# An opening without diagonals: where a graph-attention kernel makes its first norms, sums and shifts

## The reference

```
h  = relu(layernorm(x))
s  = (h @ W) @ a1 + ((ent @ W) @ a2).T          # 4096 x 4096
e  = where(adj > 0, leaky_relu(s, 0.2), -9e15)
x  = x + elu(softmax(e, axis=1) @ ent + h)
h  = relu(layernorm(x))
out = x + (adj == 1) @ h + h
```

## Time and profile before

| | us |
|---|---|
| median of 3 runs | 394.81 |
| lowest, highest | 394.11, 399.67 |
| profiled execution | 395.57 |
| its span in the profile | 393.8 |
| TensorE busy | 347.1 |
| VectorE busy | 302.9 |
| ScalarE busy | 189.3 |
| GpSimd busy | 123.8 |

### The profile page before, as it was taken

How to read it: one execution, slowest core, us unless ns; L and a number is a source line. 1 busy time by engine, 2 the same in 40 slices (tenths; PEclk the granted TensorE clock), 3 DMA queues, 4 the chain that set the end, 5 groups by cost and what they waited for, 6 DMA issues and landing times.

```text
span 393.8 us, 5685 instructions
## 1 busy us (share of the span) xinstructions
PE 347.1 (88%) x2327; PEld 122.8 (31%) x2327; DVE 302.9 (77%) x334; ACT 189.3 (48%) x241; POOL 123.8 (31%) x164
## 2 busy tenths in 40 slices
PE   1598397999867988899897999998989999999996
PEld 0345111223211221233222433332323333334564
DVE  2813889999889998989899589899897898922211
ACT  1131255776556655635745555445656555522100
POOL 4299993111111114134511311111114399000400
PEclk9989879999999999999998999999999999999999
DMA  7999969999797966765699567999999960000011
GB/s 208 257 213 213 213 126 212 213 213 214 151 136 128 160 124 106 146 108 90 117 135 153 95 112 95 109 108 108 107 103 107 107 68 2 0 2 2 1 55 53
DMA packets 15850, 47.92 MB, mean 122 GB/s; under 512 B 1553, under 2 KB 1617, under 8 KB 15569
## 3 DMA queue, kind: packets, MB, share of 16 engines
q0 software_dynamic: 14656, 44.05, 72.0%
q1 hardware_dynamic: 1168, 3.52, 2.5%
HBM read 111.53 MB, written 1.05 MB: 286 GB/s over the span
## 4 chain that ended last, share of the span: by engine, by line
PE 43%; DVE 16%; issue 5%; ACT 3%; POOL 1%; DVEq 0%; ACTq 0%
PE pb L1161 14%; PE pb L1082 9%; PE pa L1082 8%; PE pb L1176 8%; DVE yp L870 7%; DVE am L780 5%; ACT yp L642 2%; PE pa L1053 1%; PE pa L978 1%; PE pa L1047 1%; POOL rstd L497 1%; DVE gmax L742 1%; PE pa L1043 1%; DVE ta L811 1%; DVE ta L810 1%
## 5 line engine op out<-in xcount | busy, mean ns | idle before, releaser
L642 ACT ACTIVATE yp<-yp,tbias 128x1024 f32<-128x1024 f32 (+1 forms) x160 | 151.6, 977 | 109.7 <-DVE yp L870 108.4
L870 DVE SCALAR_TENSOR_TENSOR yp<-s8b,t8neg,am 128x1024 f32<-128x1024 f32 (+1 forms) x160 | 164.6, 1076 | 20.2 <-PE pb L1176 19.0
L1161 PE MATMUL pb<-yp,enta 128*64 128x512 f32 x512 | 138.0, 622 | 26.4 <-ACT yp L642 26.2
L422 POOL DMA_DIRECT2D am<-adj_t x64 | 35.2, 557 | 126.9 <-DVE yp L870 126.6
L780 DVE TENSOR_TENSOR am<-am,vx 128x4096 uint16<-128x4096 uint16 x32 | 73.5, 2298 | 1.2 <-ACT vx L556 1.2
L1176 PE MATMUL pb<-yp,onesf 128*32 128x512 f32 x512 | 68.5, 607 | 0.0
L1161 PEld LDWEIGHTS pb<-yp,enta 128*64 128x64 f32 x512 | 28.6, 137 | 93.2 <-ACT yp L642 68.0
L1082 PE MATMUL pb<-am,h 128*64 128x512 bf16 (+1 forms) x432 | 55.8, 383 | 0.0
L1082 PEld LDWEIGHTS pb<-am,h 128*64 128x64 bf16 x432 | 26.5, 111 | 40.3 <-issue 29.6
L431 POOL DMA_DIRECT2D am<-adj_t x16 | 11.5, 717 | 61.4 <-DVE yp L870 61.4
L1082 PE MATMUL pa<-am,h 128*64 128x512 fp8e4 x240 | 28.2, 380 | 0.0
(11 more groups left out here) (160 smaller groups left out, 254.9 us busy)
## 6 DMA issues: line engine op xcount, KB each, us to landing
am<-adj_t POOLq DMA_DIRECT2D x80, 512.0 KB, 9.7
edge<-adj_t POOLq DMA_DIRECT2D x4, 512.0 KB, 9.8
enta<-ent SPq DMA_DIRECT2D x1, 1040.0 KB, 5.3
xs<-xt SPq DMA_DIRECT2D x1, 1024.0 KB, 11.8
out<-yp SPq DMA_DIRECT2D x4, 256.0 KB, 2.0
mats<-eye SPq DMA_DIRECT2D x1, 320.0 KB, 7.3
wt_sb<-w_t SPq DMA_DIRECT2D x1, 32.0 KB, 2.2
a_sb<-a_cols SPq DMA_DIRECT2D x1, 0.5 KB, 2.0
```

The costliest lines, as they stand in the source:

```text
L422: pool.dma_start(am[:, q % RING], adj_t[q]).then_inc(landed[q % RING], 16)
L642: e = sc.activation(y, y, ACT.Exp, bias=tbias[:, at:at + 1])
L870: y = v.scalar_tensor_tensor(out=yp[:, n % YS, r * HALF:r * HALF + W], in0=s8b[:, pair(b) % 2, cols(b)], scalar=t8neg[:, at:at + 1], in1=a ...
L1161: t.matmul(acc2(b)[s * D:(s + 1) * D, :], enta[:, at, 0:D], yp[:, n % YS, s * HALF:(s + 1) * HALF], start=(jt == 0), stop=final, tile_posi ...
```

## The change

- `spread_out` becomes `deviations_first`: GpSimd makes the root alone, no diagonals. `deviation` on TensorE now multiplies the root's column, repeated 64 times as weights, by the identity: eight products of 128 columns for a pair instead of two of 512 columns. The squares go to a part of `h3` (`sq0`) instead of `yp`, so that the steps may use `yp` while they are needed.
- The norms of pairs 2 and 3 move. Their centring and variance stand behind `v_rows(0, 0)`, mixed with the sums `biggest(1, 0..2)`; their `deviation` in steps 1 and 3, and their `normed` behind `y` of steps 4 and 6 (`NORM`). The banks of `pb` are assigned anew (`bank_n`), and the denominators' first product waits for `normed(1)`.
- The column sums of the entities are made in three parts (`column_sums`), two products ahead of `biggest(0, 7)`, three ahead of `turn(0, 0)` and three ahead of `v_rows(0, 0)`, in a bank of their own (`esums`). `turn(0, 0)` no longer waits for their copy.
- GpSimd issues chunks 4 to 17 at once, then makes the roots of pairs 0 and 1, issues chunks 18 to 23, makes the roots of pairs 2 and 3, and then splits the sums.
- Block 1's sums: `biggest(1, 0..2)` stand ahead of step 0, and the estimate of landing changes, so that k = 3 falls on step 0, and k = 4 to 7 on steps 1 to 4 (before: k = 0 to 4 on step 0, and 5 to 7 on steps 1 to 3). `read_sums(1)` moves from step 4 to step 5, and turn, largest, shifts and rows of block 1 each by one step.
- `LONE_AT` goes from 6 to 12, and `lone_rows` of block 1 on VectorE no longer waits for block 0's products.

The diff, cut to its core:

```diff
-        n = max(0, int(q * 1.29 - 15.5)) if q < 32 else 0
+        n = min(24, max(0, int(q * 1.27 - 14.2))) if q < 32 else 0
...
-    LONE_AT = 6
+    LONE_AT = 12
+    NORM = {2: dict(dev=1, h=4), 3: dict(dev=3, h=6)}
...
+        def bank_n(p):
+            return pb[:, (2, 0, 1, 3)[p]]
+        esums = pb[:, 3, 0:4 * (D + 1)]
... GpSimd
-            def spread_out(p):
+            def deviations_first(p):
                 pool.wait_ge(var0_sb, p + 1)
                 link(g.tensor_scalar(rstd0[:, p], rstd0[:, p], 1.0, EPS, ALU.mult, ALU.add))
-                link(g.tensor_tensor(rstd0[:, p], rstd0[:, p], mhalf[:], ALU.pow))
-                g.tensor_tensor(yp[:, p].rearrange("p (t k) -> p t k", k=P),
-                                eyef.unsqueeze(1).to_broadcast([P, 2 * SUB, P]),
-                                rstd0[:, p].unsqueeze(2).to_broadcast([P, 2 * SUB, P]), ALU.mult).then_inc(sd_ready, 1)
-            for q in range(4, 8):
+                g.tensor_tensor(rstd0[:, p], rstd0[:, p], mhalf[:], ALU.pow).then_inc(sd_ready, 1)
+            for q in range(4, 18):
                 load(q)
-            for p in range(NP):
-                spread_out(p)
-                for q in range(8 + 2 * p, 10 + 2 * p):
-                    load(q)
-            for q in range(16, 18):
+            deviations_first(0)
+            deviations_first(1)
+            for q in range(18, RING):
                 load(q)
+            deviations_first(2)
+            deviations_first(3)
... (the split of the sums)
-            for q in range(18, RING):
-                load(q)
... ScalarE
+            for p in range(2):
+                squares_first(p)
+                variances_first(p)
             s_rows(0)
             s_cols(range(0, 1))
+            v_rows(0, 0)
             act.wait_ge(esum_ps, 1)
-            sc.copy(ta[:, 0:4 * (D + 1)], turned[:, 0:4 * (D + 1)]).then_inc(esum_sb, 1)
-            v_rows(0, 0)
+            sc.copy(ta[:, 0:4 * (D + 1)], esums).then_inc(esum_sb, 1)
+            for p in range(2, NP):
+                squares_first(p)
+                variances_first(p)
... VectorE
-                if b >= 1:
+                if b >= 2:
                     dve.wait_ge(pv_done, start_of[b - 1] + LONE_AT + 2)
...
+                for p, f in NORM.items():
+                    if n == f["h"]:
+                        normed(p)
... TensorE
-                for s in range(2):
-                    mm = t.matmul(pb[s * D:(s + 1) * D, p], onesf[:, 0:D], yp[:, p, s * HALF:(s + 1) * HALF],
-                                  start=True, stop=True, tile_position=(0, s * D))
+                for c in range(SUB):
+                    for s in range(2):
+                        k = s * SUB + c
+                        mm = t.matmul(bank_n(p)[s * D:(s + 1) * D, c * P:(c + 1) * P],
+                                      rstd0[:, p, k:k + 1].to_broadcast([P, D]), eyef,
+                                      start=True, stop=True, tile_position=(0, s * D))
...
+            def column_sums(places):
+                for k in places:
+                    mm = t.matmul(esums, onesf[:], enta[:, 4 * k:4 * k + 4].rearrange("p t d -> p (t d)"),
+                                  start=(k == 0), stop=(k == NT // 4 - 1))
... (the new order; only its lines)
             centred_first(0)
             centred_first(1)
             variance(0)
+            pe.wait_ge(gtab_ready, 1)
+            biggest(0, 0)
             variance(1)
+            biggest(0, 1)
             deviation(0)
+            biggest(0, 2)
             s_rows(0)
             s_cols(0)
+            biggest(0, 3)
             deviation(1)
+            for k in range(4, NQ - 1):
                 biggest(0, k)
+            column_sums(range(0, 2))
+            biggest(0, NQ - 1)
+            column_sums(range(2, 5))
             turn(0, 0)
+            column_sums(range(5, NT // 4))
             v_rows(0, 0)
+            biggest(1, 0)
+            centred_first(2)
+            centred_first(3)
+            biggest(1, 1)
+            variance(2)
+            biggest(1, 2)
+            variance(3)
... (in the steps, behind the products of step n)
+                for p, f in NORM.items():
+                    if n == f["dev"]:
+                        deviation(p)
...
-                    if jt == 1 and b >= 1:
-                        pe.wait_ge(den_sb, 2 * b)
+                    if jt == 1:
+                        if b >= 1:
+                            pe.wait_ge(den_sb, 2 * b)
+                        else:
+                            pe.wait_ge(h0_ready, 2)
```

More of the change, by code:

```diff
@@ L231, in graph_layers @@
         arep = am[0:D, 22].bitcast(F32)[:, 0:P]
+        sq0 = h3[:].rearrange("p t d -> p (t d)").bitcast(F32)[:, 0:NP * HALF].rearrange("p (q i) -> p q i", i=HALF)
         def chunks_of(p, j):
@@ L611, in move_out, with squares_first, variances_first @@
                 sc.copy(part[:, k], pb[:, 3]).then_inc(part_ready, 1)
-            for p in range(NP):
+            def squares_first(p):
                 act.wait_ge(x0_ps, p + 1)
-                sc.activation(yp[:, p, 0:HALF], pb[:, p], ACT.Square).then_inc(x0_sq, 1)
-                sc.activation(h0[:, p], pb[:, p], ACT.Relu).then_inc(x0_relu, 1)
+                sc.activation(sq0[:, p], bank_n(p), ACT.Square).then_inc(x0_sq, 1)
+                sc.activation(h0[:, p], bank_n(p), ACT.Relu).then_inc(x0_relu, 1)
+            def variances_first(p):
                 act.wait_ge(var0_ps, p + 1)
@@ L691, in normed @@
                 dve.wait_ge(x0_relu, p + 1)
-                v.tensor_tensor(h0[:, p], h0[:, p], pb[:, p], ALU.mult).then_inc(h0_ready, 1)
+                v.tensor_tensor(h0[:, p], h0[:, p], bank_n(p), ALU.mult).then_inc(h0_ready, 1)
             dve.wait_ge(ld_w, 32)
@@ L849, in _ @@
             read_sums(0)
-            normed(2)
             largest(0, 0)
@@ L854, in _ @@
             lone_rows(0)
-            normed(3)
             for n in range(STEPS_ALL):
@@ L927, in variance @@
                     pe.wait_ge(var0_sb, p)
+                if p >= 2:
+                    pe.wait_ge(vx_ready, 1)
                 for c in range(SUB):
                     at = (p * SUB + c) * 2
-                    mm = t.matmul(rowp[:, at:at + 2], yp[:, p, c * P:(c + 1) * P], mean2, start=True, stop=True)
+                    mm = t.matmul(rowp[:, at:at + 2], sq0[:, p, c * P:(c + 1) * P], mean2, start=True, stop=True)
                 mm.then_inc(var0_ps, 1)
@@ L945, in s_rows @@
                 if p == 0:
-                    pe.wait_ge(var0_sb, NP)
+                    pe.wait_ge(var0_sb, 2)
                     pe.wait_ge(gtab_ready, 1)
@@ L986, in turn @@
                 pe.wait_ge(s8_ready, 2 * (pair(b) + 1))
-                if b == 0:
-                    pe.wait_ge(esum_sb, 1)
-                else:
+                if b >= 1:
                     pe.wait_ge(um_ready, first[b])
@@ L1002, in v_rows @@
                     pe.wait_ge(vx_ready, 1)
+                    pe.wait_ge(var0_sb, NP)
                 for c in range(SUB):
@@ L1088, in neighbours @@
                     mm.then_inc(piece_done, 1)
+            def column_sums(places):
+                for k in places:
+                    mm = t.matmul(esums, onesf[:], enta[:, 4 * k:4 * k + 4].rearrange("p t d -> p (t d)"),
+                                  start=(k == 0), stop=(k == NT // 4 - 1))
+                if NT // 4 - 1 in places:
+                    mm.then_inc(esum_ps, 1)
             def centred_first(p):
-                t.matmul(pb[:, p], centre, xs[:, p], start=True, stop=True).then_inc(x0_ps, 1)
+                if p == 3:
+                    pe.wait_ge(esum_sb, 1)
+                t.matmul(bank_n(p), centre, xs[:, p], start=True, stop=True).then_inc(x0_ps, 1)
             pe.wait_ge(ld_eye, 16)
@@ L1104, in _ @@
             variance(0)
-            centred_first(2)
+            pe.wait_ge(gtab_ready, 1)
+            biggest(0, 0)
             variance(1)
-            centred_first(3)
-            variance(2)
-            variance(3)
+            biggest(0, 1)
             deviation(0)
-            pe.wait_ge(gtab_ready, 1)
-            for k in range(2):
-                biggest(0, k)
+            biggest(0, 2)
             s_rows(0)
             s_cols(0)
[L1116 to L1123, removed]
+            biggest(0, 3)
             deviation(1)
-            for k in range(3, NQ):
+            for k in range(4, NQ - 1):
                 biggest(0, k)
-            deviation(2)
+            column_sums(range(0, 2))
+            biggest(0, NQ - 1)
+            column_sums(range(2, 5))
             turn(0, 0)
+            column_sums(range(5, NT // 4))
             v_rows(0, 0)
-            deviation(3)
+            biggest(1, 0)
[5 more added lines that the diff above has]
+            variance(3)
             for n in range(STEPS_ALL):
@@ L1133, in _ @@
                 for b2 in range(1, NB):
-                    for k in range(NQ):
```

(1 more changed line is left out.)

## The result

The changed kernel takes 393.4 us at the median of 18 runs (391.78 to 396.14), the kernel before 395.93 over as many. The ratio is 0.9936, 95% interval 0.9906 to 0.9965: 2.5 us faster, where 2.9 was forecast; the time itself lies 1.5 above the forecast 391.9. Of the 18 times before, ten lie between 394.11 and 396.55 and eight between 398.88 and 400.70 (the ratio counts only the two of these under 400); the changed kernel has no such second group, and against the ten alone it is 1.8 us faster in the mean (394.95 and 393.13). The profiled execution has a span of 391.6 us against 393.8.

A forecast was written before the change was run, and what follows sets the result against it. VectorE was taken as the bound, a queue behind the first `y`. That starts 6.25 us earlier, less 1.2 of added products and waits of VectorE: 2.9 gained at the tenth `y`, 391.9 against median 394.81; range 388.5 to 397.5.

The forecast's parts named there:

- What bounds it and where the gain ends: Whole kernel: VectorE works off a queue behind the first `y`; 6.25 us earlier there, 2.9 left at tenth `y` and end.
- The diagonals: Pair 0's norm: without diagonals the root is ready at 22.05 instead of 24.0; the new `deviation` takes 1.3 us.
- The path to the largest sums: Opening, from pair 0's root to `read_sums(0)`: the landing at 30.2 sets `biggest(0, 7)`; 31.0 instead of 36.71.
- The rival for the low clock: Opening and loop: TensorE at half clock makes small products dearer; gain between 1.5 and -2, 395 us; chance 10%.
- The first steps: Steps 0 to 9: VectorE waits 1.1 before the fifth `y`, 2.1 before `read_sums(1)`, and does two products of 0.6.
- rival 1: Roots of pairs 2 and 3 held off by VectorE's scores: fifth `y` 3.1 us later, 395.0 us; chance 13%.
- its variant: Roots of pairs 2 and 3: a running root also holds VectorE, 2 x 1.67 us, giving 395.2 us; chance 3%.
- rival 4: Opening: GpSimd's queue doesn't hold so many loads, so `biggest(0, 7)` comes 12.5 us later, 404.4 us; chance 7%.
- The loads: Chunk 18 issued by 27 us instead of 56.24, closing a 3.2 us gap; nobody on the path waits, costed at nothing.
- the step that failed: `lone_rows` at step 12: the same products six steps later, waiting for the split; costed at nothing.

The follow-up runs named there:

- e2: Changed kernel with both deviations and products of pairs 2 and 3 finished ahead of step 0 again; median 397.91 us.
- e1: Changed kernel with the deviations of pairs 2 and 3 in steps 5 and 7, their VectorE products in 8 and 10; median 393.82 us.
- e4: Changed kernel plus eight unused bf16 products in TensorE's wait for the first exponential; median 392.43 us.
- e5: Changed kernel with the old landing estimate, so `read_sums(1)` is in step 4 again; median 394.46 us.
- e6: Changed kernel with chunks 18 to 23 issued behind the split of the sums and after `y` of step 5; median 393.38 us.
- e9: Changed kernel with `LONE_AT` 12 for block 0 only and 6 for the other blocks; median 393.09 us.
- e10: Changed kernel with `LONE_AT` 6 behind block 0 and eight unused products in TensorE's wait for the first exponential; median 391.20 us.
- e11: e10 with the deviations of pairs 2 and 3 in steps 5 and 7, their VectorE products in 8 and 10; median 390.22 us.
- e8: Changed kernel with GpSimd's diagonals and the old `deviation` again for pairs 0 and 1; median 398.95 us.
- e12: e11 plus unused products from 4.7 us on in TensorE's waits through the opening; median 389.59 us.
- e3: Changed kernel with the entities' column sums in one block ahead of `biggest(0, 3)` instead of three parts; median 400.48 us.
- e7: Changed kernel plus eighteen unused products of ones while TensorE waits for its first data, from 4.7 us on; median 394.38 us.

## Why the prediction was right

*What bounds it and where the gain ends.* Right. The first `y` moved by 5.7 us (forecast 6.25), 2.14 were left at the tenth `y` (2.9), and 2.2 at the end. e2 gives the same from the other side. How near the number came is in part luck, as two profiles are compared: the same opening list put the first `y` between 38.50 and 41.33 in eight profiles (changed, e1, e4, e5, e6, e9, e10 and e11), with chunk 7 landing between 29.9 and 30.3 in all of them. That spread is the clock's.

*The diagonals.* Right: root ready near 22.3, pitch at full clock 1.02, the lower bound; I had taken 1.3. e8 shows what they cost: 1.0 of start, and at least 2.3 in the times.

*The path to the largest sums.* The term mis-sized is the clock. I had the landing at 30.2 setting the time and 31.05 for `read_sums(0)`; it came at 32.05, because TensorE worked at the low level until 26.7, and ran `biggest(0, 7)` 1.3 us behind the landing (30.2, as I had it). In e4, e6, e9 and e11, where the clock rose at 18 to 19, the same list gave 30.55 to 30.93. The rival for the low clock was there with a chance of 10%; a part of it happened. From `read_sums(0)` to the first `y` it took 7.95 and not 8.4, which gave back 0.45 of the 1.0.

*The first steps.* Two terms were off and cancelled, which is luck. The fifth `y` waited 2.55, not 1.1, since I counted the loop at full clock; e4, which keeps it, measured 1.1. `read_sums(1)` waited 0.6, not 2.1, as VectorE came later to it; in e11, where it came early, it waited 2.0. Their sum is 3.15, forecast 3.2. The two products on VectorE cost 0.6 each, as said.

*GpSimd.* Right. Its operations for pairs 2 and 3 took 0.75, 2.05, 0.43 and 2.02 beside VectorE's scores and none was held for long; the cast's 7.91 in the earlier trace rows was not repeated, so rival 1 fell, and with it its variant, since a running root didn't hold the scores. The queue took all loads: when chunk 17 was issued at 17.7, only chunks 0 and 1 had landed, so sixteen transfers were outstanding, and rival 4 fell.

*The loads* cost and gain nothing: e6.

*`lone_rows`* is the step that failed: "Nothing", for placing it at step 12. I looked at the condition that was removed and not at the constant in the one that stays, which moved from step 23's denominators to step 29's. It costs 1.6 when the clock is low there (e1, e4), and nothing otherwise, as in the changed kernel's own profile, where the wait was 1.0 for ScalarE.

## What to carry to other kernels

Where a list starts late, follow the first item of the bounding engine and add up that engine's waits until it is saturated; what is left there is what arrives at the end. A constant that is shared by a place and by a wait is two edits: read each use. In a latency chain of small matrix products, price TensorE at both levels of its clock, and read more than one profile: the same list came out up to 2.8 us apart here. Cheap products in TensorE's waits can keep the clock up; ahead of the first steps eight of them brought 1.5 us (e4), and in an opening that the landing of a chunk sets they brought the first `y` no earlier (e12 against e11).

## What the runs showed of the hardware

With the same list, TensorE's clock rose at 26.7 in the changed kernel's profile, at 18.0 in e6 and only behind 29.5 in e3 (at 32.9). Eighteen products in the first 14 us went with a clock that was full from 8.9 and low again from 19.2 to 26.0 (e7); with eighteen more in the waits from 10 to 28 us it stayed full until 111 (e12). A low stretch of 3.4 us cost 1.6 to 1.9 us behind step 32 (273.1 to 273.4 against 271.5), and nothing near 113 once no wait of VectorE hung on the products in it (e10, e12). GpSimd issued fourteen transfers of 512 KB back to back, 0.54 us each, with sixteen outstanding at 17.7, and seventeen at 28.1 after six more, with no limit showing. Powers of 128 x 8 took 2.0 beside VectorE's scores and 1.67 without, and the scores took no longer by them.
